# Attention feeding a mixture of experts: values between score pairs, reciprocals spread by one DMA, statistics one row earlier

## The reference, cut to what matters

```python
def xcond(q, k, v, k_length):                      # q = layernorm(x); k = v = ctx; batch 16, 8 heads of 16 rows
    s = SCALE * jnp.log(k_length)[:, None, None, None]
    attn = jnp.einsum('bhdq,bhdk->bhqk', qh, kh)   # 512 queries, 512 keys
    attn = jax.nn.softmax(s * attn, axis=-1)
    return jnp.einsum('bhqk,bhdk->bhdq', attn, vh).reshape(b, hd, lq)
...
x = x + xcond(layernorm(x), ctx, ctx, lengths)     # x is (16, 128, 512)
x = x + ffn(layernorm(x), gate_w, w1, w2, w3)      # top 2 of 8 experts for each of 2048 tokens
```

## Time and profile before

| | us |
|---|---|
| median of 3 runs (1242.59 to 1244.8) | 1244.6 |
| the profiled execution's own time | 1244.34 |
| its span | 1242.8 |
| busy PE / DVE / ACT / POOL over the span | 1071.0 / 817.7 / 409.6 / 617.0 |
| of the stretch 329 to 360 (31 us, about one slot): PE / DVE / ACT / POOL | 29.13 / 24.58 / 20.53 / 19.68 |

### The profile page before, as it was taken

How to read it: one execution, slowest core, us unless ns; L and a number is a source line. 1 busy time by engine, 2 the same in 40 slices (tenths; PEclk the granted TensorE clock), 3 DMA queues, 4 the chain that set the end, 5 groups by cost and what they waited for, 6 DMA issues and landing times.

```text
span 1242.8 us, 19948 instructions
## 1 busy us (share of the span) xinstructions
PE 1071.0 (86%) x5113; PEld 419.8 (34%) x5114; DVE 817.7 (66%) x969; ACT 409.6 (33%) x734; POOL 617.0 (50%) x564
## 2 busy tenths in 40 slices
PE   1799999999999999861999999999999999999910
PEld 0223333333333333210444444444444444444400
DVE  5977877777777877313673864947768395953255
ACT  3266666666666666741111111110011101111100
POOL 6453666666666662123660752816657083840045
PEclk9999999999999999985999999999999999999965
DMA  6564555555555543013673755846657565753377
GB/s 172 161 216 149 169 156 158 158 164 161 164 164 164 164 135 102 21 37 109 200 166 87 216 144 143 220 93 194 168 178 178 142 186 146 215 134 83 71 226 257
DMA packets 210919, 191.65 MB, mean 154 GB/s; under 512 B 137376, under 2 KB 176288, under 8 KB 205472
## 3 DMA queue, kind: packets, MB, share of 16 engines
q1 hardware_dynamic: 196704, 119.86, 37.2%
q0 software_dynamic: 14176, 71.31, 17.5%
HBM read 107.50 MB, written 52.95 MB: 129 GB/s over the span
## 4 chain that ended last, share of the span: by engine, by line
PE 60%; POOL 11%; DMA 10%; DVE 7%; issue 6%; ACT 4%; POOLq 1%; SPq 1%; DVEq 0%; ACTq 0%
PE rows L1085 23%; PE heads_out L1085 12%; PE heads_out L999 7%; PE rows L972 6%; PE scores L986 6%; POOL W L429 6%; DMA W<-parts_dram 5%; ACT W L603 3%; DVE nm L720 3%; POOL W L428 3%; PE misc L1048 2%; DMA U<-expert_out_dram,fidx 2%; PE misc L1069 1%; PE misc L1025 1%; DMA U<-wpack_dram 1%
## 5 line engine op out<-in xcount | busy, mean ns | idle before, releaser
L1085 PE MATMUL rows<-W,U 128*128 (+1 forms) x1776 | 391.1, 380 | 23.4 <-DMA U<-stage 19.5
L720 DVE TENSOR_REDUCE nm<-rows 128x2 f32<-128x1024 f32 x256 | 305.3, 1219 | 59.6 <-PE rows L972 49.7
L603 ACT ACTIVATE W<-scores 128x512 f32<-128x512 f32 x512 | 282.7, 597 | 162.6 <-PE scores L986 157.2
L1085 PEld LDWEIGHTS rows<-W,U 128*128 128x128 bf16 x1776 | 174.1, 98 | 235.4 <-issue 29.3
L666 ACT ACTIVATE U<-rows 128x512 f32<-128x512 f32 x78 | 46.4, 597 | 517.8 <-PE rows L1085 509.0
L1085 PE MATMUL heads_out<-W,U 128*128 x888 | 197.8, 379 | 12.6 <-issue 10.2
L972 PE MATMUL rows<-W,U 96*128 96x512 bf16 x512 | 163.8, 404 | 49.2 <-DMA W<-parts_dram 28.1
L986 PE MATMUL scores<-U,W 128*128 128x512 bf16 x512 | 179.5, 386 | 14.0 <-ACT W L603 4.9
L429 POOL TENSOR_TENSOR W<-U,W 128x2048 bf16<-128x2048 f32 x42 | 172.4, 4104 | 7.7 <-POOL W L428 7.7
L910 DVE TENSOR_TENSOR U<-rows,U 128x512 f32<-128x512 f32 x78 | 53.5, 686 | 175.8 <-ACT U L666 175.8
L917 DVE TENSOR_TENSOR U<-U 128x512 bf16<-128x512 f32 x78 | 162.8, 2087 | 2.7
(11 more groups left out here) (150 smaller groups left out, 697.3 us busy)
## 6 DMA issues: line engine op xcount, KB each, us to landing
U<-wpack_dram POOLq DMA_DIRECT2D x42, 1024.0 KB, 5.8
parts_dram<-U SPq DMA_DIRECT2D x32, 384.0 KB, 4.1
U<-parts_dram SPq DMA_DIRECT2D x32, 384.0 KB, 4.0
W<-parts_dram SPq DMA_DIRECT2D x32, 384.0 KB, 5.5
stage<-slots_dram SPq DMA_DIRECT2D x39, 256.0 KB, 3.0
expert_out_dram<-U SPq DMA_DIRECT2D x39, 256.0 KB, 3.1
parts_dram<-U SPq DMA_DIRECT2D x32, 256.0 KB, 4.0
stage<-wpack_dram POOLq DMA_DIRECT2D x12, 512.0 KB, 5.3
```

What stands on the lines that cost most here:

```text
L603: s.activation(probs[:, w % 2, j, kk, :], sc[u % 2][:, :], ACT.Exp) \
L720: v.tensor_reduce(nm[:, bb.parity, 2 * k:2 * k + 2], p1[k % 2][:, :].rearrange("p (c k) -> p c k", c=2), AX_X, ALU.max, negate=True).then_ ...
L1085: ins = m.matmul(bank, part_of(s_part, k), W[:, bass.ds(at_w, 512)], start=(k == 0 and n == 0), stop=(k == n_chunks - 1 and n == 2))
```

## The change

Five edits, all in the attention's slots.

1. On PE the 16 rows units stand in pairs between score groups: unit 4w at u = 0, 4w+1 behind u = 3, 4w+2 before u = 4, 4w+3 behind u = 7. The values then stand between two pairs of scores with no rows unit beside them.
2. The matmul that spreads the reciprocals, `selb`, `r8` and DVE's multiplication into `tb` go. One DMA from `recips_dram` writes each head's row to its 16 partitions of a full tile `rb` (256 KB instead of 16 KB), and POOL multiplies `us` by it in place, then adds `xres` in place.
3. ACT's copy into `us` waits for the z of the batch before; its copy of the residual back to `xres` moves from between exponentials 4 and 5 of group 3 to the end of the slot.
4. POOL's scatter of z moves from before the four keys steps to behind them.
5. DVE's statistics move from behind maxima 14 to behind maxima 13 of the slot.

```diff
-                    sp.dma_start(r8[:, :], recips_dram[bass.ds(pv.n, 1)].rearrange("o h q -> (o h) q")) \
-                        .then_inc(S["rec_in"], 16)
+                    sp.dma_start(rb[:, :], recips_dram[bass.ds(pv.n, 1)].rearrange("o h q -> (o h) q")
+                                 .unsqueeze(1).to_broadcast([H, DH, L])).then_inc(S["rec_in"], 16)
...
-                pv2 = b.plus(-2)
-                if pv2.within(0, B - 1):
-                    hold(S["idx_ready"], b.n - 1)
-                    for a in range(2):
...
                     high_low(st, pt[:, 4, :], pt[:, 5, :], rest[:, :])
                     st.end()
+                pv2 = b.plus(-2)
+                if pv2.within(0, B - 1):
+                    hold(S["idx_ready"], b.n - 1)
+                    for a in range(2):
...
+                    hold(S["us_ready"], b.n)
+                    hold(S["rec_in"], b.n * 16)
+                    g.tensor_tensor(us[:, :], us[:, :], rb[:, :], ALU.mult).then_inc(S["t_ready"], 1)
                     hold(S["t_ready"], b.n)
-                    if pv.within(1, B - 1):
-                        hold(S["x1_kept"], b.n - 1)
                     xr = xres[:, bass.ds(pv.n, 1), :].rearrange("p o q -> p (o q)")
-                    g.tensor_tensor(x1[:, :], xr, tb[:, :], ALU.add).then_inc(S["x1_ready"], 1)
+                    g.tensor_tensor(us[:, :], xr, us[:, :], ALU.add).then_inc(S["x1_ready"], 1)
...
                     if pv.within(1, B - 1):
-                        act.wait_ge(S["t_ready"], b.n - 1)
+                        act.wait_ge(S["z_ready"], b.n - 1)
+                        s.nop().then_inc(S["act_held"], 1)
+                        act.wait_ge(S["x1_kept"], b.n - 1)
                     s.activation(us[:, :], misc[:, :], ACT.Copy).then_inc(S["us_ready"], 1)
...
-                    v.tensor_tensor(tb[:, :], misc[:, :], us[:, :], ALU.mult).then_inc(S["t_ready"], 1)
-                maxima(range(13, 15))
-                if b.within(-2, -2):
-                    number()
+                maxima(range(13, 14))
                 if pv.within(0, B - 1):
                     dve.wait_ge(S["x1_ready"], b.n)
...
-                    v.bn_stats(st2[:, :], x1[:, :]) \
+                    v.bn_stats(st2[:, :], us[:, :]) \
...
                     v.bn_aggr(mv2[:, :], st2[:, :]).then_inc(S["st2_ready"], 1)
+                maxima(range(14, 15))
...
                 for w in range(4):
                     for u in range(8):
-                        if u % 2 == 0:
+                        if u % 4 == 0:
                             rows_unit(4 * w + u // 2)
                         if full:
                             score(w, u)
...
-                            m.matmul(misc[:, :], selb[:, :], r8[:, :], start=True, stop=True).then_inc(S["r_ready"], 1)
-                            reader = (S["t_ready"], b.n)
+                        if u % 4 == 3:
+                            rows_unit(4 * w + u // 2)
```

More of the change, by code:

```diff
@@ L122, in build @@
         us = sb("us", [P, L], F32)
[L123 to L124 removed]
+        rb = sb("rb", [P, L], F32)
         z = sb("z", [P, 2, D], F32)
@@ L224, in slots @@
                 body(Batch(b // 2, b % 2, b, b))
-        N_CONST = 10
+        N_CONST = 9
         block = cx.enter_context(nc.Block())
@@ L516, in slot @@
                     st.step(g.tensor_scalar(zsc[:, 2:3], mv2[:, 0:1], -1.0, 0.0, ALU.mult, ALU.add))
-                    st.step(g.tensor_scalar(z[:, pv.parity, :], x1[:, :], zsc[:, 2:3], zsc[:, 1:2], ALU.add, ALU.mult))
+                    st.step(g.tensor_scalar(z[:, pv.parity, :], us[:, :], zsc[:, 2:3], zsc[:, 1:2], ALU.add, ALU.mult))
                     st.end()
@@ L640, in slot @@
                 exps(3, range(0, 5))
-                if behind:
+                exps(3, range(5, 8))
+                if pv.within(0, B - 1):
                     act.wait_ge(S["x1_ready"], b.n)
-                    s.activation(xres[:, bass.ds(pv.n, 1), :].rearrange("p o q -> p (o q)"), x1[:, :], ACT.Copy) \
+                    s.activation(xres[:, bass.ds(pv.n, 1), :].rearrange("p o q -> p (o q)"), us[:, :], ACT.Copy) \
                         .then_inc(S["x1_kept"], 1)
-                exps(3, range(5, 8))
             slots(act, slot)
@@ L830, in slot @@
                     v.bn_aggr(mv2[:, :], st2[:, :]).then_inc(S["st2_ready"], 1)
+                maxima(range(14, 15))
+                if b.within(-2, -2):
+                    number()
                 maxima(range(15, 16))
@@ L1002, in values @@
                         ins.then_inc(S["pv_done"], 1)
-                reader = (S["t_ready"], b.n - 1) if pv2.within(0, B - 1) else \
-                    (S["m_ready"], b.n + 1) if full else None
+                reader = (S["m_ready"], b.n + 1) if full else \
+                    (S["rank_used"], b.n - 2) if b.within(B + 1, B + 1) else \
+                    (S["us_ready"], b.n - 1) if b.within(B, B) else None
                 for w in range(4):
                     for u in range(8):
-                        if u % 2 == 0:
+                        if u % 4 == 0:
                             rows_unit(4 * w + u // 2)
@@ L1064, in slot @@
                             reader = (S["m_ready"], b.n + 2)
-                        if (w, u) == (3, 1) and behind:
-                            pe.wait_ge(S["rec_in"], b.n * 16)
-                            if reader:
-                                pe.wait_ge(*reader)
-                            m.matmul(misc[:, :], selb[:, :], r8[:, :], start=True, stop=True).then_inc(S["r_ready"], 1)
-                            reader = (S["t_ready"], b.n)
+                        if u % 4 == 3:
+                            rows_unit(4 * w + u // 2)
             slots(pe, slot)
```

28 lines of the change are left out of this document (8 added, 20 removed).

## The result

| | us |
|---|---|
| changed kernel, median of 4 runs (1227.33 to 1232.27) | 1228.4 |
| kernel before beside it, median of 4 runs (1242.59 to 1244.8) | 1243.7 |
| ratio, with its 95% interval | 0.9884 [0.9867, 0.9902] |
| the profiled execution of the changed kernel | 1232.27, span 1230.7 |

The change is worth 1.2%, some 15 us; 19.5 were forecast.

What follows compares the result with a forecast made beforehand. PE's bad order bound the slot, DVE nearly full; afterwards the reciprocals' chain, 26.75 + r (3.2), sets 30.0 us instead of 31.16. Gains 15.5 + 2 + 2 = 19.5; 1244.4 - 19.5 = 1225, range 1207 to 1246.

Steps and rivals of the forecast that it cites:

- the first rival: Attention slots: the forecast itself, slot 29.6 to 30.4 us, time 1220 to 1231; chance 0.44.
- Reload to rb, 7.08: SP's queue: from the reload's issue to the return DMA's issue 7.08 us, untouched by the change.
- r, 3.2 with 0.25 to wake: Return DMA: rb lands 3.2 us after its issue (2.7 to 4.8), then POOL takes 0.25 to wake.
- The 16th score, 14.1: PE: the 16th score ends 14.1 us after the slot's first rows unit, 16.75 before.
- Multiply to statistics, 2.86: POOL to DVE: multiply 1.28, hand-over 0.2, add 1.28, wake of DVE 0.1.
- behind the statistics 1.0 + 1.16 + 0.1: Slot's end: statistics 1.0, unit 14's maxima 1.16, then 0.1 until PE may start the next slot's unit 0.
- rival 2: DVE's floor: rb lands by 2.1 or the chain starts sooner, slot 28.85 us, time 1209; chance 0.20.
- rival 3: DVE's routing held up by POOL's keys: two collisions of 1.05 us per slot, time 1237; chance 0.12.
- rival 5: Slower, rb lands late: r 4.8 to 5.2, slot 31.75 us, time 1249; r of 4.4 reaches 31.16; chance 0.15.
- The ends: Attention's first and last slots: slot 0 gains 2 us from the order, slots 14 and 15 gain 2.
- the two new waits: DVE at the statistics on POOL's x1, 0.5 to 1 us; PE at unit 0 on DVE, 1 to 1.5.
- cut to less than half: Attention's waits: ACT's on scores and the loads' on ACT fall below half of their earlier size.

Runs made afterwards that it cites:

- early_recips: Changed kernel with DVE's reciprocal behind maxima 5 instead of 6 and its store ahead of the reload on SP; ratio to the kernel before 0.9793, 1221.8 us.
- rows16: Changed kernel with the reciprocals stored twice in DRAM, so the return DMA reads 16 rows instead of 8; ratio to the kernel before 0.9922, 1238.4 us.
- stats_back: Changed kernel with the statistics put back behind maxima 14 (edit 5 undone); ratio to the kernel before 0.9917, 1235.2 us.
- order_only: Kernel before with edit 1 alone, the new order on PE; ratio to the kernel before 0.9967.
- early_stats_back: Changed kernel with the reciprocal behind maxima 5, its store ahead of the reload, and the statistics back behind maxima 14; ratio to the kernel before 0.9871.
- scatter_first: Changed kernel with POOL's scatter of z back in front of the keys steps (edit 4 undone); ratio to the kernel before 1.0162, 1269.2 us.
- old_order: Changed kernel with PE's rows units back in front of every second score (edit 1 undone); ratio to the kernel before 1.0228, 1274.3 us.
- changed_again: The changed kernel itself, unaltered, run again on another chip; ratio to the kernel before 0.9867, 1229.3 us.

## Why the prediction was right, and where it was off

The direction and the mechanism held: faster, with a chain through rb, x1 and the statistics that sets the slot. 1225 was forecast, 1228.4 came, within the first rival's own range. That the chain sets the slot is shown from both sides: early_recips shortens it and gains 7.5 us, and the same edit in the kernel before gains nothing.

**The slot, step by step**, counted from the z transposes (forecast / mean of slots 2 to 13): rb issued 19.2 / 18.8, multiplication 22.65 / 22.9, statistics 25.5 / 25.8, next transposes 29.95 / 30.20. Two terms were off, by 0.6 down and by 0.65 up. That they cancel is luck, and the slot came out closer than its parts.

- *Reload to rb, 7.08*: it measures 6.5 in the mean and 5.9 in the good slot. I carried the row of one slot over as a constant; it is the time that a 16 KB store spends behind 768 KB, and it varies from slot to slot, with 4.35 to 6.36 from store to return in slots 2 to 13.
- *r, 3.2 with 0.25 to wake*: 4.1 from issue to multiplication in the mean, and 4.25 where POOL waited. The middle of 2.7 and 3.7 was too low. The rule that the prediction weighed against it, 8 rows at half the engines (the Trainium skill, DMA: Bandwidth & Descriptors, Why a DMA increments its semaphore by 16 and not by 1), made an estimate of 3.3 of it: the right direction, as rows16 shows, and still too low. (Its 1.2 us of moving comes to 1.1 at the rate that it takes; nothing hangs on that.)
- *The 16th score, 14.1*: 14.36 in the good slot (337.62 + 0.22 - 323.48). Near enough.
- *Multiply to statistics, 2.86; behind the statistics 1.0 + 1.16 + 0.1*: 2.83 and 4.44 - 2.19 = 2.25. Right.
- *z behind the statistics* was a second path that I did not write down: 3.96 to the transposes. It does not bind in the changed kernel (4.44 by the other path); it does in stats_back, order_only and early_stats_back.

**The floor of DVE, 28.85** (rival 2): the best slots are 29.2 to 29.8 in early_recips, 29.45 in the mean. Laying out the order by hand missed some 0.6. The routing operations took 0.7 more of DVE's time than before, which may be all of it; no run shows that. So rival 2 had a limit of about the right size, and the changed kernel comes down to it in some slots.

**DVE held up by GpSimd** (rival 3): the meetings occur, at some 0.7 us of DVE's time per slot and not 2.1. **Slower** (rival 5): r comes to 3.9 in the mean (4.11 less the wake-up) where 4.4 would have decided, with the reload's delay as I took it; that one is shorter. scatter_first and old_order end up slower than the kernel before. (Rival 5's sum gives 1248, not 1249.)

**The ends.** Of the 19.5 us forecast the attention gave 15.6: slots 2 to 13 gave 12.3, with slot 1 and half of slot 14 they were to give 15.5, and slots 14 to 16 gave 3.3 for the 2 forecast. Slot 0 was to gain 2 and lost 2.6: the transpose of `nm` in it is at 76.88 instead of 74.28. By the first z transposes that was made good, and no more (113.19, before 113.26). In this profile the granted clock from 50 to 60 us is 0.50, and in that of before 1.00:

```profile
50.00:60.00 10.00, 8.22 (x18) 1.80 (x17) 8.16 (x8) 3.10 (x6) 0.41 (x1) 0.50 0.72 209
```

That figure doesn't tell the two apart: a rows unit takes 0.85 instead of 0.44 in both, in the kernel before up to 59 us, in the changed one up to 62. Behind that, PE waits 0.91 for DVE at 69.09 and 1.24 for a reload at 76.22, and before it waited for neither. The ten profiles with the new order have this transpose at 75.3 to 78.4, the three with the old one at 73.7 to 74.8, with either clock on record among the ten. So the new order costs something in slot 0, which the forecast had as a gain; why stays open. The experts' phase is 3.5 longer in this one profiled execution, which lies at the upper end of its four runs.

**The signs to look for.** Right were the two new waits and their places. Wrong was "cut to less than half" for the loads' wait on ACT. The saving of 2.1 us on PE is there in the slot that I compared, in the spacing of matmuls, and the row that I chose can't show it.

## What to carry to other kernels

Where several engines feed each other, each edit is worth only what the next limit leaves: of an order that frees 2.1 us on PE, 0.35 came through alone, 0.6 with the scatter and the statistics moved, and 1.0 to 1.25 with the DMA route as well; without that order the rest was a loss of 2.3%. When a chain becomes the bound, look at its DMAs' places in their queue first: a 16 KB transfer that feeds another one belongs ahead of the big transfer beside it, even where the second then queues behind it. And cost a lateness on PE with what follows: here a stand of 2 to 3.6 us was in most cases followed by matmuls at half clock, for another 0.6 to 1.9 us.

## What the hardware did that I had not expected

- *The clock after a stand.* At the head of slots 3 to 14, PE stood for 1.9 us or more in 30 cases. The values behind it took 1.4 to 1.87 instead of 1.00 in 24 of them: 10 of 11 in old_order, 10 of 12 in scatter_first, 3 of 3 in rows16, 1 of 1 in changed_again and none of 3 in the changed kernel. The granted clock was 0.50 to 0.81 in the stretches of 3 to 4 us read above (1.00 being 2.4 GHz, 0.50 1.2), and in the 24 cases the z transposes came 0.6 to 1.9 us later than without it. It isn't the wait's length alone: behind 2.88 in the changed kernel and behind 3.40 in scatter_first they took 1.00, and behind 1.94 in rows16 1.87.
- *A small store behind large loads.* 16 KB to DRAM and the wait for it take 4.1 to 6.6 us when issued behind 768 KB on the same queue, and 2.0 to 2.8, with the reload's issue in between, when issued ahead of them in the changed kernel. The store itself lands in 1.4 to 2.0 us there, and in 4.0 to 6.5 behind the reload in the kernel before.
- *One source row for many partitions.* With the 256 KB from 8 rows the multiplication starts 3.7 to 4.6 us behind the issue (mean 4.12), from 16 rows 3.4 to 3.95 (mean 3.65); SP takes 0.71 to issue the one where the 16 KB took 0.30.
